# Last attention stage with two convolutions first, FFN transposes on two PSUM banks, shorter softmax bookkeeping

## The chip, the cores and the metric

The kernel runs on one core of a Trainium2 chip. The metric is the device time of one execution in microseconds, 1619.86 us before the change (median of 3 runs). The engines are TensorE (PE, with weight loads shown as PEld), VectorE (DVE), ScalarE (ACT), GpSimd (POOL) and the sync engine (SP), which here issues every DMA.

## The reference, cut to what matters

```
x  = x + attn(cond(x, c))            # stage A: per-sample mixing, then a state-space block
x  = x + ffn(cond2(x, c))            # stage B, the part touched, with the end of stage A

attn:  proj = h @ in_proj.T;  xBC = silu(causal conv of 4 taps)
       y = scan over 32 positions + x * D          # 64 heads in 8 groups
       yn = y * rsqrt(mean over the group of y*y + eps) * norm_weight * silu(gate)
       out = yn @ out_proj.T
cond2: conv1d(x, weight, 9 taps, 4 groups of 8 channels) + c @ c_weight.T + bias
ffn:   dots = softmax(x @ centroids.T / 0.1)       # 64 clusters
       hits = dots > 0.01
       query_sel = any(hits, axis=1);  row_sel = any(hits, axis=0)[assignments]
       out = where(query_sel & row_sel, x @ weight.T + bias, 0)
```

## The kernel before, in words

The 2048 rows (64 samples of 32 channels, 512 wide) lie in SBUF as 16 tiles of 128 rows, `acc[:, T]`. Every float32 product of the large matmuls is taken as three products of a high and a low part (`oh`/`ol`, `yh`/`yl`, `xh`/`xl`, `wh`/`wl`): ACT copies the high part out, DVE or POOL subtracts to get the low one.

Stage A is a loop over 32 stages n (a weight group by a half of the positions). A stage projects ten times on PE, and in the stage after it the four tiles i of stage n are finished: `Y(n, i)` (L675, the decay-weighted products on PE), `y_dve` (L692 y, L700 y times gate, on DVE), `y_high` (L719, ACT), `y_low` (L735, POOL), `y_square` (L711, ACT), `y_sum` (L726 and L730, POOL), `S` (L743, PE), `rstd` (L751 DVE, L756 POOL), `O(n, i)` (L775, twelve matmuls on PE, needs `yh` and `yl` of the tile) and `add_out` (L788, DVE). `A_dve` (L645) and `M_dve` (L655) on DVE make `dtx` and `Mb`, which `Y` reads. Stage 31 has no stage after it. `last_products` does this work, mixed with the start of stage B.

Stage B runs over the 16 tiles T. The updated rows are stored to HBM (`x2s`, L961) and loaded back shifted (`load_G`, L976, four DMAs of about 260 KB a tile); `conv2(T)` (L1058) and `conv2_last_tap` (L1066) are the convolution, always two tiles together; `x3_act` (L1076, ACT) adds the bias; `turn(T)` (L1085) transposes the tile in four pieces into PSUM bank `PT`; `x3_split` (L1094 ACT, L1096 DVE) makes high and low parts; `ffn(T, c)` (L1121, twelve matmuls) multiplies, c=1 the right 224 columns with the 64 cluster columns, c=0 the left 288; `ffn_ops` on DVE and ACT does the softmax over the clusters (L1147 row maximum, L1149 scale, L1154 exp on ACT, L1135 `dense` that copies the product out with its bias, L1159 reciprocal, L1161 scaling, L1164 running maximum `pmx`, L1165 row maximum, L1167 row mask `qs`). Up to tile 9 both halves of a tile are multiplied in its turn; from tile `LATE` = 10 only c=1 is, and the c=0 halves follow when the cluster mask is known: `ffn(10, 0)`, a transpose of `pmx` (L1253), its maximum and threshold (L1255, L1257), and two one-hot matmuls that spread the mask over the columns (L1261, L1262). After those, DVE and POOL put the masked results into `acc` (L1278, L1286, L1289, L1297, L1299) and SP stores them (L1272).

Nothing is scheduled by a planner: each engine runs its instructions in the order in which the Python calls append them to its queue, and waits at the written `wait` lines for an event of another engine, or of itself. So the order of calls in `last_products` and `second` is the order on every engine at once. SP's queue before the conv loads of tiles 0, 2, 1, 3 holds nothing of this place: `load_G(1)` and `load_G(3)` wait for projection 8 of stage 31, and the loads of tiles 4 and 5 for the convolutions of tiles 0 and 1, whose buffers they overwrite.

The names of PSUM banks: `PT` = 6 and `PG` = 3; `PG` holds the scan's small products and the sums of `S` until `rstd` has read them.

Of the kernel before, what the change touches and what calls it, by code (L numbers as in the profile page):

```python
# [10 lines left out]
AX = mybir.AxisListType  # L11

NT = 16
# [43 lines left out]
def adaln_attn_ffn_kernel(nc, x, emb, gin, b2, wbank, biask, w_in, w_dt, w_out, prm, cst, cw4, ctxw,  # L57
                          w_ffn, b_ffn, asg, x2s, out):
    ctx = ExitStack()
    with ctx:  # L60
# [58 lines left out]
        pmx = gmt[:, 2, :]  # L119
# [957 lines left out]

        def turn(T):
            pe.wait("x3", T)
            if T >= 1:  # L1080
                pe.wait("x3l", T - 1)
            else:
                pe.wait("dtx", (end_n, 3))
            for k in range(4):
                fn = lambda e, k=k: e.transpose(PS[:, PT, 128 * k:128 * k + 128], xs[:, T % 2, 128 * k:128 * k + 128], ident)  # L1085
                pe.op(fn, "xt", T) if k == 3 else pe.op(fn)

        def x3_split(T):
            act.wait("xt", T)
            if T >= LATE:  # L1090
                act.wait("O", (end_n, 3))
            elif T >= 3:
                act.wait("ff", (T - 3, 0))
            act.op(lambda e: e.copy(x3_slot(True, T), PS[:, PT, :]), "x3h", T)  # L1094
            dve.wait("x3h", T)
            dve.op(lambda e: e.tensor_tensor(x3_slot(False, T), PS[:, PT, :], f(x3_slot(True, T)), ALU.subtract), "x3l", T)  # L1096

        FB = ((SEG[0], PP[2]), PY)

# [37 lines left out]
        def ffn_ops(T):  # L1137
            r = T % 2
            banks = FB[r]
            lgt = PS[:, banks[1], 224:288]  # L1140
            nm, sx, rc = s4[:, 2 + r:3 + r], s4[:, 4 + r:5 + r], s4[:, 6 + r:7 + r]
            d = spots[T]
            dve.wait("ff", (T, 1))
            if T >= 1:
                dve.wait("fn", T - 1)
                dve.wait("q", T - 1)
            dve.op(lambda e: e.tensor_reduce(s4[:, 0:1], lgt, AX.X, ALU.max), "fm", T)  # L1147
            dve.wait("fm", T)
            dve.op(lambda e: e.tensor_scalar(nm, s4[:, 0:1], -10.0, None, ALU.mult), "fn", T)  # L1149
            act.wait("fn", T)  # L1150
            if T >= 2:
                act.wait("pm", T - 2)
                act.wait("qm", T - 2)
            act.op(lambda e: e.activation(ex[:, r, :], lgt, ACT.Exp, bias=nm, scale=10.0, accum_out=sx), "se", T)  # L1154
            dve.wait("ld_bf", 0)
            if T < LATE:
                dense(T, 0)
            dense(T, 1)
            dve.op(lambda e: e.reciprocal(rc, sx), "frc", T)  # L1159
            dve.wait("frc", T)  # L1160
            dve.op(lambda e: e.tensor_scalar(ex[:, r, :], ex[:, r, :], rc, None, ALU.mult), "pp", T)  # L1161
            dve.wait("pp", T)
            dve.wait("pm", T - 1)
            dve.op(lambda e: e.tensor_tensor(pmx, pmx, ex[:, r, :], ALU.max), "pm", T)  # L1164
            dve.op(lambda e: e.tensor_reduce(s4[:, 1:2], ex[:, r, :], AX.X, ALU.max), "qm", T)  # L1165
            dve.wait("qm", T)
            dve.op(lambda e: e.tensor_scalar(qs[:, T:T + 1], s4[:, 1:2], 0.01, None, ALU.is_gt), "q", T)  # L1167
            dve.wait("q", T)
            if T >= LATE:
                return  # L1170
            if T < APART:
                dve.op(lambda e: e.tensor_scalar(d, d, qs[:, T:T + 1], None, ALU.mult), "res", T)
                return
            dve.op(lambda e: e.scalar_tensor_tensor(out=d, in0=d, scalar=qs[:, T:T + 1], in1=acc[:, T, 4:516],
                                                    op0=ALU.mult, op1=ALU.add), "res", T)
# [23 lines left out]
        def last_products():  # L1199
            n = end_n  # L1200
            conv2(0)
            y_dve(n, 0)
            y_high(n, 0)
            y_low(n, 0)
            y_square(n, 0)
            y_sum(n, 0)
            A_dve(n, 2)
            A_dve(n, 3)
            M_dve(n, 2)
            M_dve(n, 3)  # L1210
            for i in (1, 2, 3):
                y_dve(n, i)
                y_square(n, i)
                y_sum(n, i)
                y_high(n, i)
                y_low(n, i)
            weights2(0)
            weights2(1)
            O(n, 0)
            Y(n, 2)  # L1220
            Y(n, 3)
            O(n, 1)
            S(n, (0, 1))
            conv2(1)
            conv2_last_tap(0)
            x3_act(0)
            load_G(4)
            load_G(5)
            O(n, 2)
            turn(0)  # L1230
            O(n, 3)
            S(n, (2, 3))
            x3_split(0)
            weights2(2)
            weights2(3)
            x3_act(1)
            for tiles in sums(n):
                rstd(n, tiles)
                for i in tiles:
                    add_out(n, i)  # L1240

        for n in range(NS):
            stage(n)
# [13 lines left out]
        dve.op(lambda e: e.tensor_scalar(csel, bc(sm[:, 40:41], 64, 128), 0.01, None, ALU.is_gt), "cs", 1)  # L1257
        pe.wait("cs", 1)
        pe.wait("oh1", 0)
        pe.wait("var", (end_n, 3))  # L1260
        pe.op(lambda e: e.matmul(PS[:, PG, :], csel, ohf, start=True, stop=True), "rsel", 0)  # L1261
        pe.op(lambda e: e.matmul(PS[:, PT, :], csel, ohf, start=True, stop=True), "rsel2", 0)  # L1262
        for T in range(LATE + 1, NT):
# [138 lines left out]
```

How the kernel before makes its waits and increments, by code:

```python
    def emit(self, eng, sems):  # L43
        seen = {}
        for it in self.items:
            if it[0] == "wait":
                v = self.book[it[1]][it[2]]
                if seen.get(it[1], 0) < v:
                    eng.wait_ge(sems[it[1]], v)
                    seen[it[1]] = v
            else:
                ins = it[1](eng)
                if it[2] is not None:
                    ins.then_inc(sems[it[2]], it[3])
```

## Time and profile before

| | us |
|---|---|
| median of 3 runs (1619.21 to 1621.07) | 1619.86 |
| the profiled execution, its own time | 1624.18 |
| its span, first to last instruction | 1622.4 |
| PE busy in the span | 1594.5 |
| stage 31's leftover work and first convolutions | about 1494 to 1521 |
| FFN turns | about 1521 to 1602 |
| mask, masked sums and stores | about 1602 to 1622 |

The span and the device time are of one profiled execution; the runs that the change is measured against have a median 4.3 us shorter than that execution. PE is busy for nearly all of the span, so a change shows where PE stands idle, and in the last 20 us, where PE is no longer the last to finish.

### The profile page before, as it was taken

The numbers are of one execution on the slowest core, as the hardware profiler recorded it, in microseconds if no ns is written. First come the engines' busy times: TensorE is split into PE (matmuls) and PEld (weight loads), VectorE is DVE, ScalarE is ACT, GpSimd is POOL, SyncE is SP. The second block draws the span as 40 slices with busy tenths as digits, with TensorE's granted clock in tenths as the row PEclk, the third lists the DMA queues.
The fourth block names the chain that finished last, engine by engine and source line by source line (L and its number), as shares of the span: only waits on it lengthen the run. The fifth ranks groups of instructions, "written<-read, shape, count | busy, mean of one in ns | idle before, by whom it ended". The sixth has DMA issues, their size and how long they took to land. (4 is left out here: it accounts for less than half of the span.)

```text
span 1622.4 us, 32566 instructions
## 1 busy us (share of the span) xinstructions
PE 1594.5 (98%) x13001; PEld 1279.6 (79%) x13001; DVE 1055.4 (65%) x1741; ACT 846.1 (52%) x1372; POOL 774.1 (48%) x731
## 2 busy tenths in 40 slices
PE   9999999999999999999999999999999999999997
PEld 6778888888888888877787888888888888887665
DVE  4877666665656666676786656565666666565456
ACT  3654556555555555555455655555454655554321
POOL 3564545546363644544345554636464554543203
PEclk9999999999999999999999999999999999999999
DMA  5110201111111102011012111111010201115782
GB/s 184 59 53 21 59 21 58 35 53 40 40 53 34 49 15 63 27 53 40 30 43 73 53 40 46 47 34 60 33 40 21 65 27 53 41 36 116 190 187 105
DMA packets 50294, 93.19 MB, mean 57 GB/s; under 512 B 5664, under 2 KB 6304, under 8 KB 50144
## 3 DMA queue, kind: packets, MB, share of 16 engines
q1 hardware_dynamic: 50144, 91.11, 19.5%
q8 instruction: 104, 1.70, 0.4%
q14 instruction: 46, 0.38, 0.1%
HBM read 82.64 MB, written 8.45 MB: 56 GB/s over the span
## 5 line engine op out<-in xcount | busy, mean ns | idle before, releaser
L487 PE MATMUL PS<-xh,wh 128*128 128x512 f32 x1280 | 519.6, 406 | 0.0
L487 PE MATMUL PS<-xh,wl 128*128 128x512 f32 x1280 | 499.8, 390 | 0.0
L487 PE MATMUL PS<-xl,wh 128*128 128x512 f32 x1280 | 499.8, 390 | 0.0
L522 DVE SCALAR_TENSOR_TENSOR cb<-PS,P,cb 128x496 f32<-128x496 f32 (+2 forms) x576 | 412.5, 716 | 132.4 <-ACT cb L508 118.8
L184 POOL TENSOR_TENSOR wl<-rw,wh 128x512 fp32r<-128x512 f32 x160 | 212.2, 1331 | 191.6 <-ACT wh L179 191.6
L726 POOL TENSOR_TENSOR ysum<-yq 128x256 f32<-128x256 f32 x128 | 109.5, 856 | 362.3 <-ACT yq L711 362.2
L487 PEld LDWEIGHTS PS<-xh,wl 128*128 128x128 f32 x1280 | 240.3, 188 | 52.9
L487 PEld LDWEIGHTS PS<-xh,wh 128*128 128x128 f32 x1280 | 240.6, 188 | 50.7 <-ACT wh L179 0.5
L487 PEld LDWEIGHTS PS<-xl,wh 128*128 128x128 f32 x1280 | 241.1, 188 | 44.4
L508 ACT ACTIVATE cb<-PS,P 128x512 f32<-128x512 f32 x192 | 148.4, 773 | 204.9 <-PE PS L487 204.9
L775 PE MATMUL PS<-oh,yh 128*128 128x512 f32 x512 | 200.1, 391 | 3.2 <-POOL yl L735 3.2
L655 DVE TENSOR_TENSOR big<-Lt,gmt 128x512 f32<-128x512 f32 x128 | 102.6, 843 | 153.3 <-ACT Lt L588 153.3
L775 PE MATMUL PS<-oh,yl 128*128 128x512 f32 x512 | 199.2, 389 | 0.0
L775 PE MATMUL PS<-ol,yh 128*128 128x512 f32 x512 | 199.2, 389 | 0.0
L711 ACT ACTIVATE yq<-y 128x512 f32<-128x512 f32 x128 | 81.0, 633 | 207.5 <-DVE y L692 201.2
L512 ACT ACTIVATE big<-PS 128x512 f32<-128x512 f32 x128 | 76.2, 595 | 147.9 <-PE PS L487 147.5
L542 ACT ACTIVATE big<-cb 128x512 f32<-128x512 f32 x192 | 119.6, 623 | 62.7 <-DVE cb L522 62.5
L788 DVE SCALAR_TENSOR_TENSOR acc<-PS,rs,acc 128x512 f32<-128x512 f32 x128 | 93.1, 749 | 84.0 <-issue 45.9
L756 POOL TENSOR_TENSOR rs<-vr,mh 128x1 f32<-128x1 f32 (+1 forms) x95 | 56.9, 599 | 168.6 <-DVE vr L751 168.5
L645 DVE TENSOR_TENSOR dtx<-PS,dtt 128x512 f32<-128x512 f32 x128 | 82.1, 682 | 59.9 <-PE PS L612 59.7
L775 PEld LDWEIGHTS PS<-oh,yh 128*128 128x128 f32 x512 | 96.1, 188 | 24.7 <-issue 5.1
L775 PEld LDWEIGHTS PS<-oh,yl 128*128 128x128 f32 x512 | 96.1, 188 | 20.0
(201 smaller groups left out, 2184.1 us busy)
## 6 DMA issues: line engine op xcount, KB each, us to landing
rw<-in_w_in SPq DMA_DIRECT2D x160, 256.0 KB, 2.7
ro<-in_w_out SPq DMA_DIRECT2D x64, 256.0 KB, 2.8
x2s<-acc SPq DMA_DIRECT2D x16, 260.0 KB, 5.3
out_x<-acc SPq DMA_DIRECT2D x16, 256.0 KB, 2.4
acc<-in_x SPq DMA_DIRECT2D x3, 1024.0 KB, 9.9
wh<-x2s SPq DMA_DIRECT2D x8, 260.0 KB, 3.4
wl<-x2s SPq DMA_DIRECT2D x8, 260.0 KB, 6.4
wh<-x2s SPq DMA_DIRECT2D x8, 259.5 KB, 4.2
```

Source lines behind the costliest of these rows:

```text
L184: pool.op(lambda e: e.tensor_tensor(wl[:, m, :], rw[:, q % RW, :], f(wh[:, m, :]), ALU.subtract), "w_lo", (u, m))
L487: fn = lambda e, k=k, w=w, v=v, i=i: e.matmul(PS[:, bank, :], w[:, m, 128 * k:128 * k + 128], v[:, k, a:a + 512], start=(i == 0), stop=(i ...
L508: act.op(lambda e: e.activation(cb[:, z % 2, :], PS[:, bank, :], ACT.Identity, bias=P[:, P_CB + c:P_CB + c + 1], scale=P[:, P_CW + 4 * c + ...
L512: act.op(lambda e: e.activation(gate[:, m - 6, :], PS[:, bank, :], ACT.Silu), "ev", (n, m))
L522: dve.op(lambda e, d=d, w=w: e.scalar_tensor_tensor(out=cv[:, :, d:32], in0=pv[:, :, 0:32 - d], scalar=w, in1=cv[:, :, d:32], op0=ALU.mult ...
L542: act.op(lambda e: e.activation(dst, cb[:, z % 2, :], ACT.Silu), "silu", (n, m))
L645: dve.op(lambda e: e.tensor_tensor(dtx[:, r, :].rearrange("p (j v c) -> p j v c", j=4, v=2), PS[:, b0:b0 + 2, 256 * r:256 * r + 256].rearr ...
L655: dve.op(lambda e: e.tensor_tensor(Mb[:, r], bc(Lt[:, 256 * i:256 * i + 256].rearrange("p (h o t) -> p h o t", h=8, o=1), 128, 8, 2, 32), ...
L711: act.op(lambda e: e.activation(yq[:, :], y[:, r, :], ACT.Square), "yq", (n, i))
L726: pool.op(lambda e: e.tensor_tensor(ysum[:, :], yq[:, 0:256], yq[:, 256:512], ALU.add), "ys1", (n, i))
L775: fn = lambda e, j=j, v=v, w=w, q=q: e.matmul(PS[:, O_bank(n, i), :], v[:, r, 128 * j:128 * j + 128], w[:, j, :], start=(q == 0), stop=(q ...
L788: dve.op(lambda e: e.scalar_tensor_tensor(out=acc[:, T, 4:516], in0=PS[:, O_bank(n, i), :], scalar=rs[:, i:i + 1], in1=acc[:, T, 4:516], o ...
```

## The change

`last_products` is rewritten: both first convolutions and their last tap come ahead of the first `O`, the elementwise work is done in pairs of tiles (0, 1) and (2, 3), the first transposes come before `O` of tile 2, and the splits of the FFN weights come after the second tile's output. `turn` writes to `PT` and `PG` in turn, and so waits for the split of the tile two before and not one before. In `ffn_ops` the scaling by the reciprocal and the running maximum are one instruction; the row mask is taken from the reciprocal itself (the largest exponential of a row is 1, so the largest softmax value is the reciprocal); and for the last tile `dense(15, 1)` is issued after the running maximum.

```
--- before.py
+++ after.py
@@ -1077,12 +1077,12 @@
 
         def turn(T):
             pe.wait("x3", T)
-            if T >= 1:
-                pe.wait("x3l", T - 1)
+            if T >= 2:
+                pe.wait("x3l", T - 2)
             else:
-                pe.wait("dtx", (end_n, 3))
+                pe.wait(*(("dtx", (end_n, 3)), ("var", (end_n, 3)))[T])
             for k in range(4):
-                fn = lambda e, k=k: e.transpose(PS[:, PT, 128 * k:128 * k + 128], xs[:, T % 2, 128 * k:128 * k + 128], ident)
+                fn = lambda e, k=k: e.transpose(PS[:, (PT, PG)[T % 2], 128 * k:128 * k + 128], xs[:, T % 2, 128 * k:128 * k + 128], ident)
                 pe.op(fn, "xt", T) if k == 3 else pe.op(fn)
 
         def x3_split(T):
@@ -1091,9 +1091,9 @@
                 act.wait("O", (end_n, 3))
             elif T >= 3:
                 act.wait("ff", (T - 3, 0))
-            act.op(lambda e: e.copy(x3_slot(True, T), PS[:, PT, :]), "x3h", T)
+            act.op(lambda e: e.copy(x3_slot(True, T), PS[:, (PT, PG)[T % 2], :]), "x3h", T)
             dve.wait("x3h", T)
-            dve.op(lambda e: e.tensor_tensor(x3_slot(False, T), PS[:, PT, :], f(x3_slot(True, T)), ALU.subtract), "x3l", T)
+            dve.op(lambda e: e.tensor_tensor(x3_slot(False, T), PS[:, (PT, PG)[T % 2], :], f(x3_slot(True, T)), ALU.subtract), "x3l", T)
 
         FB = ((SEG[0], PP[2]), PY)
 
@@ -1143,28 +1143,26 @@
             dve.wait("ff", (T, 1))
             if T >= 1:
                 dve.wait("fn", T - 1)
-                dve.wait("q", T - 1)
             dve.op(lambda e: e.tensor_reduce(s4[:, 0:1], lgt, AX.X, ALU.max), "fm", T)
             dve.wait("fm", T)
             dve.op(lambda e: e.tensor_scalar(nm, s4[:, 0:1], -10.0, None, ALU.mult), "fn", T)
             act.wait("fn", T)
             if T >= 2:
                 act.wait("pm", T - 2)
-                act.wait("qm", T - 2)
             act.op(lambda e: e.activation(ex[:, r, :], lgt, ACT.Exp, bias=nm, scale=10.0, accum_out=sx), "se", T)
             dve.wait("ld_bf", 0)
             if T < LATE:
                 dense(T, 0)
-            dense(T, 1)
+            if T < NT - 1:
+                dense(T, 1)
+            dve.wait("se", T)
             dve.op(lambda e: e.reciprocal(rc, sx), "frc", T)
             dve.wait("frc", T)
-            dve.op(lambda e: e.tensor_scalar(ex[:, r, :], ex[:, r, :], rc, None, ALU.mult), "pp", T)
-            dve.wait("pp", T)
             dve.wait("pm", T - 1)
-            dve.op(lambda e: e.tensor_tensor(pmx, pmx, ex[:, r, :], ALU.max), "pm", T)
-            dve.op(lambda e: e.tensor_reduce(s4[:, 1:2], ex[:, r, :], AX.X, ALU.max), "qm", T)
-            dve.wait("qm", T)
-            dve.op(lambda e: e.tensor_scalar(qs[:, T:T + 1], s4[:, 1:2], 0.01, None, ALU.is_gt), "q", T)
+            dve.op(lambda e: e.scalar_tensor_tensor(out=pmx, in0=ex[:, r, :], scalar=rc, in1=pmx, op0=ALU.mult, op1=ALU.max), "pm", T)
+            dve.op(lambda e: e.tensor_scalar(qs[:, T:T + 1], rc, 0.01, None, ALU.is_gt), "q", T)
+            if T == NT - 1:
+                dense(T, 1)
             dve.wait("q", T)
             if T >= LATE:
                 return
@@ -1199,45 +1197,48 @@
         def last_products():
             n = end_n
             conv2(0)
-            y_dve(n, 0)
-            y_high(n, 0)
-            y_low(n, 0)
-            y_square(n, 0)
+            conv2(1)
+            conv2_last_tap(0)
+            for i in (0, 1):
+                y_dve(n, i)
+                y_high(n, i)
+                y_low(n, i)
+                y_square(n, i)
             y_sum(n, 0)
+            y_sum(n, 1)
             A_dve(n, 2)
             A_dve(n, 3)
             M_dve(n, 2)
             M_dve(n, 3)
-            for i in (1, 2, 3):
-                y_dve(n, i)
-                y_square(n, i)
-                y_sum(n, i)
-                y_high(n, i)
-                y_low(n, i)
-            weights2(0)
-            weights2(1)
+            x3_act(0)
+            x3_act(1)
+            load_G(4)
+            load_G(5)
             O(n, 0)
             Y(n, 2)
             Y(n, 3)
             O(n, 1)
             S(n, (0, 1))
-            conv2(1)
-            conv2_last_tap(0)
-            x3_act(0)
-            load_G(4)
-            load_G(5)
+            turn(0)
             O(n, 2)
-            turn(0)
             O(n, 3)
             S(n, (2, 3))
+            for i in (2, 3):
+                y_dve(n, i)
+                y_high(n, i)
+                y_low(n, i)
+                y_square(n, i)
+            y_sum(n, 2)
+            y_sum(n, 3)
             x3_split(0)
-            weights2(2)
-            weights2(3)
-            x3_act(1)
-            for tiles in sums(n):
-                rstd(n, tiles)
-                for i in tiles:
-                    add_out(n, i)
+            rstd(n, (0, 1))
+            add_out(n, 0)
+            add_out(n, 1)
+            for k in range(4):
+                weights2(k)
+            rstd(n, (2, 3))
+            add_out(n, 2)
+            add_out(n, 3)
 
         for n in range(NS):
             stage(n)
@@ -1257,7 +1258,6 @@
         dve.op(lambda e: e.tensor_scalar(csel, bc(sm[:, 40:41], 64, 128), 0.01, None, ALU.is_gt), "cs", 1)
         pe.wait("cs", 1)
         pe.wait("oh1", 0)
-        pe.wait("var", (end_n, 3))
         pe.op(lambda e: e.matmul(PS[:, PG, :], csel, ohf, start=True, stop=True), "rsel", 0)
         pe.op(lambda e: e.matmul(PS[:, PT, :], csel, ohf, start=True, stop=True), "rsel2", 0)
         for T in range(LATE + 1, NT):
```

PE in the last stage, as a difference (L675 is `Y` of tiles 0 and 1, L1058 the convolution, L1066 its last tap, L775 the first `O`; `w` is `w4`; a row with x8 is eight matmuls):

```order
 L675 MATMUL PS<-big,dtx 64x64 x32
-L1058 MATMUL PS<-wh,w 32x512 x8
+L1058 MATMUL PS<-wh,w 32x512 x16
+L1066 MATMUL PS<-wh,w 32x512 x8
 L775 MATMUL PS<-oh,yh 128x512
 L775 MATMUL PS<-ol,yh 128x512
```

The convolution of tile 1 and the last taps of both tiles now stand ahead of `O` of tile 0; before, they stood behind `O` of tile 1.

DVE in the same place (`big` in L692 is `xsd`, in L700 `gate`, in L655 the tile `Mb`; `yg` and `big` in L700 are the two buffers of `ygb`):

```order
 L692 TENSOR_TENSOR y<-PS,big 128x512
 L700 TENSOR_TENSOR yg<-y,big 128x512
-L645 TENSOR_TENSOR dtx<-PS,dtt 128x512 x2
-L655 TENSOR_TENSOR big<-Lt,gmt 128x512 x2
-L692 TENSOR_TENSOR y<-PS,big 128x512
-L700 TENSOR_TENSOR big<-y,big 128x512
+L692 TENSOR_TENSOR y<-PS,big 128x512
+L700 TENSOR_TENSOR big<-y,big 128x512
+L645 TENSOR_TENSOR dtx<-PS,dtt 128x512 x2
+L655 TENSOR_TENSOR big<-Lt,gmt 128x512 x2
 L692 TENSOR_TENSOR y<-PS,big 128x512
```

The y and gate products of tile 1 now come ahead of the two `A_dve` and two `M_dve`, four instructions earlier.

POOL in the same place, before:

```order
L735 TENSOR_TENSOR yl<-yg,yh 128x512
L726 TENSOR_TENSOR ysum<-yq 128x256
L730 TENSOR_TENSOR big<-ysum 128x128
L726 TENSOR_TENSOR ysum<-yq 128x256
L730 TENSOR_TENSOR big<-ysum 128x128
L735 TENSOR_TENSOR yl<-big,yh 128x512
```

and now:

```order
L735 TENSOR_TENSOR yl<-yg,yh 128x512
L735 TENSOR_TENSOR yl<-big,yh 128x512
L726 TENSOR_TENSOR ysum<-yq 128x256
L730 TENSOR_TENSOR big<-ysum 128x128
L726 TENSOR_TENSOR ysum<-yq 128x256
L730 TENSOR_TENSOR big<-ysum 128x128
```

The low part of tile 1 now stands ahead of both sums of squares.

DVE in a late FFN turn (`gmt` is `ex` or `pmx`, `s` one column of `s4`):

```order
 L1135 TENSOR_TENSOR big<-PS,pb 128x224
 L1159 RECIPROCAL s<-s 128x1
-L1161 TENSOR_SCALAR gmt<-gmt,s 128x64
-L1164 TENSOR_TENSOR gmt<-gmt 128x64
-L1165 TENSOR_REDUCE s<-gmt 128x1
-L1167 TENSOR_SCALAR qs<-s 128x1
+L1162 SCALAR_TENSOR_TENSOR gmt<-gmt,s 128x64
+L1163 TENSOR_SCALAR qs<-s 128x1
 L1096 TENSOR_TENSOR ol<-PS,oh 128x512
```

Four instructions between the reciprocal and the next tile's low part became two.

## Rows read from the trace of the kernel before

**Rows 1.** The page, part 1: busy time by engine.

```profile
PE 1594.5 (98%) x13001; PEld 1279.6 (79%) x13001; DVE 1055.4 (65%) x1741; ACT 846.1 (52%) x1372; POOL 774.1 (48%) x731
```

**Rows 2.** Windows: stretch, length, busy by engine, then clock, DMA share, GB/s.

```profile
1540.00:1560.00 20.00, 20.00 (x179) 12.71 (x179) 9.92 (x34) 5.57 (x15) 0.00 (x0) 1.00 0.97 215
```

**Rows 3.** Timeline of PE, last stage: start, duration, line, idle before in brackets.

```profile
1493.95 1.93 PE L1058 MATMUL PS<-wh,w 128*32 128x512 f32 x16
1497.60 0.47 PE L775 MATMUL PS<-oh,yh 128*128 128x512 f32 x1 [1.72 <-POOL yl L735]
...
1500.51 1.16 PE L675 MATMUL PS<-big,dtx 64*64 64x64 f32 x64
1503.18 0.47 PE L775 MATMUL PS<-oh,yh 128*128 128x512 f32 x1 [1.51 <-POOL yl L735]
...
1508.30 1.09 PE L1066 MATMUL PS<-wh,w 32*32 32x512 f32 x16
```

**Rows 4.** Timeline of DVE, last stage, and all of L700 (ns min/median/max).

```profile
1494.09 0.69 DVE L692 TENSOR_TENSOR y<-PS,big 128x512 f32<-128x512 f32 x1 [0.94 <-PE PS L675]
...
1495.42 1.28 DVE L645 TENSOR_TENSOR dtx<-PS,dtt 128x512 f32<-128x512 f32 x2
1496.62 2.58 DVE L655 TENSOR_TENSOR big<-Lt,gmt 128x512 f32<-128x512 f32 x2
...
L700 DVE TENSOR_TENSOR yg<-y,big x64: 691/692/1648, 77.7 to 1502.5; 128x512 f32<-128x512 f32 x64
```

**Rows 5.** Timeline of POOL, last stage.

```profile
1496.23 1.26 POOL L735 TENSOR_TENSOR yl<-yg,yh 128x512 fp32r<-128x512 f32 x1 [12.05 <-ACT yh L719]
```

**Rows 6.** SP issues of load_G(1), time to landing (window 1489.9:1490.4), all of `x2s`.

```profile
1488.69 1.73 SPq L976 DMA_DIRECT2D wh<-x2s  x4
...
wh<-x2s SPq DMA_DIRECT2D x1, 258.5 KB, 5.6
...
DMA to landing us min/median/max: 3.1/5.9/10.9
```

**Rows 7.** Timeline of PE, late FFN turns.

```profile
1583.52 0.63 PE L1085 MATMUL PS<-C,big 128*128 128x128 f32 x4 [0.53 <-DVE ol L1096]
1583.91 0.38 PE L1121 MATMUL PS<-xh,oh 128*128 128x288 f32 x1
...
1595.97 0.63 PE L1085 MATMUL PS<-C,big 128*128 128x128 f32 x4 [0.62 <-DVE yl L1096]
...
1598.73 0.40 PE L1121 MATMUL PS<-xh,yh 128*128 128x288 f32 x1 [0.53 <-DVE yl L1096]
...
1602.78 0.30 PE L1253 MATMUL PS<-C,gmt 128*64 128x128 f32 x1 [0.60 <-DVE gmt L1164]
```

**Rows 8.** Timeline of DVE, turns 12, 13 and 15.

```profile
1592.90 0.21 DVE L1147 TENSOR_REDUCE s<-PS 128x1 f32<-128x64 f32 x1
...
1594.27 0.26 DVE L1161 TENSOR_SCALAR gmt<-gmt,s 128x64 f32<-128x64 f32 x1
...
1595.14 0.69 DVE L1096 TENSOR_TENSOR yl<-PS,yh 128x512 fp32r<-128x512 f32 x1
...
1600.83 0.23 DVE L1147 TENSOR_REDUCE s<-PS 128x1 f32<-128x64 f32 x1
...
1601.71 0.39 DVE L1135 TENSOR_TENSOR dtx<-PS,pb 128x224 f32<-128x224 f32 x1 [0.47 <-ACT gmt L1154]
...
1602.50 0.23 DVE L1164 TENSOR_TENSOR gmt<-gmt 128x64 f32<-128x64 f32 x1
```

**Rows 9.** The chain that ended last, its end: start, us, what.

```profile
1605.80 0.60 ACT y L1305
...
1611.68 6.25 POOL acc L1289 x5
1617.93 1.22 POOLq L60
```

**Rows 10.** Window of three us, PE only: busy, clock, DMA share, GB/s.

```profile
1606.00:1609.00 3.00, 3.00 (x14) 0.50 0.45 175
```

## Prediction

> **What bounds the kernel now.** I read the page's first part, then the windows, then PE's timeline where the windows show it idle, then DVE, POOL and SP at those places, and last the chain that ended last. PE is busy for 98% of the span [rows 1], so only time in which PE stands idle, or in which something else is last, can be won. The middle of stage B has no such time: 20.00 of 20 us busy [rows 2]. The transposes of tiles 2 to 11 wait for nothing there, and the shorter DVE work of these turns is worth nothing. Two places are left.
>
> First, stage 31's leftover: PE idles 1.72 us before `O` of tile 0 and 1.51 us before `O` of tile 1, both times for the low part `yl` made on POOL [rows 3]. That is 3.23 us, and behind it PE runs without a gap to the late turns.
>
> Second, the late turns with only half a product: 0.53 us before the transpose of tile 12, 0.62 before that of tile 15, 0.53 before `ffn(15, 1)`, 0.60 before the transpose of `pmx` [rows 7]; the transpose of tile 14 has a gap like these. Each is a wait for the newest low part or for the running maximum, which DVE makes. After the mask PE is busy only because late products are left over: the chain ends in ACT's copy of the mask, POOL's sums to 1617.93 and a last 1.22 us of waiting for the store [rows 9]. That tail has unchanged operations and starts from the mask, so whatever brings the mask earlier brings the end earlier by as much.
>
> **Last stage.** PE executes the same matmuls; the second convolution (1.93 us, less 0.07 of overlap, from the first one's row) and the last taps (1.09 less 0.07) go into the first gap [rows 3]: 2.9 us of work in place of 1.72 of idling. The step needs four things.
>
> *The data of tile 1.* Its loads are issued from 1488.69 on, four within 1.73 us; the last, issued at about 1490.0, takes 5.6 us to land [rows 6], so 1495.6. The first convolution leaves PE at 1495.8. The cost is 0; the other end is a landing that is late by the semaphore's way and the other loads behind it, for which I take 0.3. What is queued behind this wait on PE is all of `O`, `Y` 2 and 3, and through them every engine.
>
> *`dtx` of tiles 2 and 3, which `O` of tile 0 waits for.* DVE's y (0.69) and gate product (0.69) of tile 1 now stand ahead of it. From 1495.42 [rows 4]: y to 1496.1, gate product to 1496.8, `dtx` twice (1.28) to 1498.1, `Mb` twice at the slow 2.58 to 1500.7. PE comes to `O` at 1495.8 + 1.86 + 1.02 = 1498.7, and to `Y` of tile 2 at 1501.6. Nothing is late. The bound is a gate product at its slowest, 1.65 us [rows 4]: 0.96 later, which makes `O` wait 0.5.
>
> *The low part of tile 1.* Its `yh` follows the gate product (1496.8) by the ACT copy, about 0.7, and `yl` takes 1.26 [rows 5], so 1498.8; `O` of tile 1 comes at 1502.7. The second gap of 1.51 goes entirely.
>
> *The low part of tile 2, next in turn to be late.* `Y` 2 and 3 end at about 1502.8, DVE starts y right behind. From y of tile 0 (1494.09 [rows 4]) to the first `O` (1497.60 [rows 3]) took 3.51 us: 1502.95 + 3.51 = 1506.46. PE, after `O` of tile 1 and the sums (3.26, from 1503.18 to the convolution 1.86 ahead of the taps at 1508.30 [rows 3]) and the transposes of tile 0 (0.39 [rows 7]), comes at 1506.45. So 0 again, with no slack; if POOL is held up, up to 0.6 is lost. The later steps (`yl` of tile 3, the split of tile 0, the rsqrt, the splits of the FFN weights, the sum of `rstd` that frees bank PG for the transpose of tile 1) come out 0.6 us or more ahead of PE by the same adding up, and their slack covers ACT's later `x3_split`.
>
> SP gains an earlier place for the loads of tiles 4 and 5 (behind the taps, 1498.7, not 1509.4). They queue behind loads and stores that are already issued, and are needed 20 us later. Nobody waits.
>
> Sum of this place: -3.23, plus 0.3 that I put in for the three slacks of a few tenths: -2.9. Bounds -3.5 (small spaces around the gaps that the modelled ends of matmuls hide) and -1.8 (0.3, 0.5 and 0.6 all paid).
>
> **Late turns.** With two banks the transposes of tiles 12 and 14 no longer wait for the low part of the tile before. They are done (0.39 from transpose to product [rows 7]) while that low part is made. That is worth 0.39 once: with tile 12, ahead of two convolutions on PE. For tile 14 the same happens, but the low part of tile 14 is held by DVE's own queue. There the step is 1592.90 to 1595.14 and again to the next [rows 8], 2.84 a turn (2.24, and 0.60 for the low part), against 2.1 for PE's transposes (0.39) and product (about 1.7, half of the 3.45 below). Of the four operations from the scaling at 1594.27 to the low part at 1595.14, 0.87 us, two remain, with one wait in place of three; I take 0.42, as half of it. The fused operation has no row: with the two remaining at a fifth of the time, 0.7 would be saved; with the fused one as dear as the two it replaces, 0.2; with all as dear as the four, nothing. Two turns (low parts of tiles 14 and 15) give 2 x 0.45 = 0.90. Then `ffn(15, 1)` starts at 1598.73 - 0.39 - 0.90 = 1597.44. Behind it stand its own product and `ffn(10, 0)`, to 1602.18 before, 3.45 us in all [rows 7], so 1600.89. The running maximum of tile 15: the maximum starts about 2.0 after the product's start (the product must be done), then before it took 1.90 (1600.83 to 1602.73 [rows 8]); less `dense` (0.39) and one of the two operations (0.27), 1.24. That is 3.24, under 3.45: PE is last, and the gap of 0.60 goes. `dense(15, 1)` falls into the 0.4 us of the transpose of `pmx`.
>
> Sum of this place: -0.39 - 0.90 - 0.60 = -1.89. Bounds: -1.0 (the two operations as long as the four) and -2.4 (0.7 twice).
>
> **Sum.** -2.9 - 1.9 = -4.8 us. From the profiled execution's 1624.18 that is 1619.4; from the median of the runs, 1619.86, which the next measurement stands against, 1615.1. This measurement can tell 0.2%, 3.2 us, from no change.
>
> **The clock.** PE's granted clock is 0.50, so 1.2 of 2.4 GHz, in 1606 to 1609 [rows 10], after PE had idled for the mask. DVE and POOL set the end there, so I put neither gain nor loss on it.
>
> **The lock.** DVE's two `Mb` products took 2.58 us beside POOL's `yl`, [rows 4, 5], against a gate product's usual 0.69 for the same size. The longest gate product, 1.65, would fit it too. As a mechanism of this kernel: of a DVE product with both inputs in SBUF and a POOL subtraction, the later waits out the earlier. Now the gate product of tile 1 (1496.1) meets `yl` of tile 0 (1496.2), and that of tile 3 (1505.0) meets `yl` of tile 2 (1505.1). If POOL wins the first, `dtx` is 0.96 late and `O` waits 0.5 to 0.8; if DVE wins the second, `yl` of tile 2 is 0.6 late and PE waits 0.5. Together the change would give 1.3 less: 1616.4. The Trainium skill, SBUF — State Buffer, "Who interferes with whom", states this rule: the port pair that VectorE and GpSimd share is an exclusive lock, and a VectorE instruction with two SBUF inputs contends with a GpSimd one that reads SBUF. By that rule the trace agrees in kind (2.58 for two); which instruction comes first is open.
>
> **The rivals.**
> - *The lock costs* at both places: 1616.4. For it the 2.58 us; against it that both meetings are within 0.1 us and may fall the good way. 14%.
> - *Another wait takes the place of the stall in the last stage*: the pairs make ACT square tile 1 only after POOL's first sum, and put tile 3's work and the split of tile 0 behind it. If the chain gate product, `yl`, sums, split, `rstd` runs 3 us late, only the late turns gain: 1618.0. Against it are slacks of 0.6 us and more. 7%.
> - *The late turns don't shorten*, because ACT's exponentials and copies are as long as DVE's row: only the first place, 1617.0. Against it, DVE waits 0.47 for ACT in a turn [rows 8] and is busy for the rest. 7%.
> - *Slower: the data of tile 1 come late.* PE now stands at the loads with everything behind it. At the longest landing of any transfer of `x2s` in the trace, 10.9 us [rows 6], they would be there at 1500.9, 5.1 after PE. A gap so long could halve the clock as it does at the end, where it is 0.50 for 3 us [rows 10] and so gives away half of that, 1.5 us. -4.8 + 5.1 + 1.5 = +1.8: 1621.7. It is slower from a landing 4.8 us late, or 3.3 with the clock. Against it stand the 5.6 us read for this very load, whose place in SP's queue is unchanged. 4%.
> - *The change doesn't do what it says*: the orders of PE, DVE and POOL do change as shown; that the time doesn't, 2%.
>
> **How the numbers follow.** The forecast holds 66%, with its own range 1614.0 to 1617.1, both places at their bounds; 3 of these 66 lie above 1616.6. Faster by over 0.2% is below 1616.6: 0.63 of the forecast and 0.09 of the lock case, 0.72. Same: the rest of both, either place lost, half of the late data, and no effect, 0.26. Slower: the other half of the late data, 0.02. The range for 8 in 10 is 1613.8, just under the forecast's own, to 1618.0, where the last stage gives nothing.
>
> **What would show it.** PE's timeline: the tap of tiles 0 and 1 ends near 1498.8 and `O` follows at once; a first gap at 1495.8 shows late data, one at 1498.8 shows `dtx`, one at 1506.5 the low part of tile 2. The first `ffn` starts near 1518.3, not 1521.2. In the late turns the low parts of DVE are 2.4 apart, not 2.84, and the transpose of `pmx` has no gap before it. A PE gap in 1520 to 1580, or POOL idle between its sums after 1606, would show me wrong.

## The result, and the profile after

The changed kernel takes 1613.53 us (median of 6 runs, 1612.93 to 1615.37), the kernel before 1619.13 in the same rounds: the ratio is 0.9965, 95% interval 0.9954 to 0.9976, so 3.9 to 7.4 us less. Timed again later it was 0.9956 (0.9943 to 0.9968). I had said 1615.1, range 1613.8 to 1618.0. The direction and both places were right. The time lies 0.27 us under the range: the change is -5.6, not -4.8, and the kernel before came out at 1619.13, the median of the three runs that I started from and three more, 0.73 below the 1619.86 that I set the change against.

The two profiled executions differ by 11.0 us of span, more than the change is worth. So I compare stretches of the program, not times from the span's start. The first convolution of the last stage starts at 1493.95 before [rows 3] and here at 1488.74, with the same code ahead of it; those 5.2 us are the start of the program, told at the end.

PE's timeline in the last stage of the changed kernel (start, duration, line, idle before in brackets), answering to [rows 3]:

```profile
1488.74 1.93 PE L1058 MATMUL PS<-wh,w 128*32 128x512 f32 x16
1491.10 1.93 PE L1058 MATMUL PS<-wh,w 128*32 128x512 f32 x16 [0.43 <-DMA wh<-x2s]
1492.96 1.09 PE L1066 MATMUL PS<-wh,w 32*32 32x512 f32 x16
1493.98 0.50 PE L775 MATMUL PS<-oh,yh 128*128 128x512 f32 x1
...
1497.99 0.50 PE L775 MATMUL PS<-oh,yh 128*128 128x512 f32 x1
...
1501.21 0.64 PE L1085 MATMUL PS<-C,big 128*128 128x128 f32 x4
1502.11 0.47 PE L775 MATMUL PS<-oh,yh 128*128 128x512 f32 x1 [0.27 <-issue]
...
1513.09 0.38 PE L1121 MATMUL PS<-xh 128*128 128x288 f32 x1
```

Both gaps of 1.72 and 1.51 are gone: the first `O` follows the taps at once, and the second follows `Y` at once. New are 0.43 of waiting for the data of tile 1 and 0.27 ahead of `O` of tile 2. From the first convolution to the first FFN product it is 24.35 us; before it was 27.25.

DVE and POOL in the same place, answering to [rows 4, 5]:

```profile
1490.93 0.69 DVE L700 TENSOR_TENSOR big<-y,big 128x512 f32<-128x512 f32 x1
...
1492.74 2.37 DVE L655 TENSOR_TENSOR big<-Lt,gmt 128x512 f32<-128x512 f32 x2
...
1500.18 0.69 DVE L700 TENSOR_TENSOR big<-y,big 128x512 f32<-128x512 f32 x1
```

```profile
1491.03 1.75 POOL L735 TENSOR_TENSOR yl<-yg,yh 128x512 fp32r<-128x512 f32 x1 [12.05 <-ACT yh L719]
1492.75 1.81 POOL L735 TENSOR_TENSOR yl<-big,yh 128x512 fp32r<-128x512 f32 x1
...
1500.28 1.73 POOL L735 TENSOR_TENSOR yl<-yg,yh 128x512 fp32r<-128x512 f32 x1 [2.49 <-ACT yh L719]
```

Twice a gate product starts 0.10 us ahead of a low part, keeps its 0.69, and the low part takes 1.75 and 1.73 in place of 1.26. The low part of tile 1 starts with the two `Mb` products, and both are long: 1.81, and 2.37 for the two.

The late turns, PE and then DVE, answering to [rows 7, 8]:

```profile
1574.66 0.60 PE L1085 MATMUL PS<-C,big 128*128 128x128 f32 x4
1575.26 0.40 PE L1121 MATMUL PS<-xh,oh 128*128 128x288 f32 x1
...
1589.15 0.40 PE L1121 MATMUL PS<-xh,yh 128*128 128x288 f32 x1 [0.51 <-DVE yl L1096]
...
1592.54 0.30 PE L1254 MATMUL PS<-C,gmt 128*64 128x128 f32 x1
```

```profile
1585.66 0.28 DVE L1162 SCALAR_TENSOR_TENSOR gmt<-gmt,s 128x64 f32<-128x64 f32 x1
1585.86 0.15 DVE L1163 TENSOR_SCALAR qs<-s 128x1 f32<-128x1 f32 x1
1586.04 0.69 DVE L1096 TENSOR_TENSOR yl<-PS,yh 128x512 fp32r<-128x512 f32 x1
...
1588.40 0.69 DVE L1096 TENSOR_TENSOR yl<-PS,yh 128x512 fp32r<-128x512 f32 x1
```

The transposes no longer wait; low parts are 2.36 apart, before 2.84; the transpose of `pmx` has no gap. From the transpose of tile 11 to that of `pmx` it is 19.98 us, before 22.05. From there to the end of POOL nothing changed. But the last wait of SP, for the last store, did. SP's waits in the last 30 us, before and after:

```profile
SPq L60 <- DMA out_x<-acc: 2.5, 1, 2.5
```

```profile
SPq L60 <- DMA out_x<-acc: 1.7, 1, 1.7
```

From POOL's end to the span's it is 3.25 us before and 2.50 after. That was in no term of my sum. The four stretches give -2.90, -0.06, -2.07 and -0.75, together -5.8.

The same stretches in every profiled execution, each worked out from that kernel's timeline. They repeat to 0.1 us where the whole time does not, but for the first, which moves with the data of tile 1. The stretch after POOL is good to 0.05, and in `e_tail`, where POOL has one sum less, it is no measure of the end:

| kernel | ratio to before, interval | first conv. to first FFN | to transpose 11 | to `pmx` | POOL's end to the end | loads on q14 |
|---|---|---|---|---|---|---|
| before | | 27.25 | 59.53 | 22.05 | 3.25 | 46 |
| before_again | | 27.25 | 59.50 | 22.06 | 3.21 | 46 |
| changed | 0.9965 (0.9954 to 0.9976) | 24.35 | 59.47 | 19.98 | 2.50 | 45 |
| after_again | 0.9956 (0.9943 to 0.9968) | 23.73 | 59.50 | 19.97 | 2.52 | 45 |
| e_stage | 0.9981 (0.9972 to 0.9990) | 24.05 | 59.47 | 22.04 | 3.25 | 46 |
| e_banks | 0.9996 (0.9987 to 1.0005) | 27.26 | 59.53 | 21.59 | 3.24 | 46 |
| e_softmax | 0.9986 (0.9977 to 0.9994) | 27.27 | 59.47 | 20.85 | 2.47 | 45 |
| e_dense | 0.9999 (0.9990 to 1.0008) | 27.29 | 59.51 | 21.74 | 3.24 | 46 |
| e_conv | 0.9992 (0.9983 to 1.0001) | 25.35 | 59.52 | 22.06 | 3.31 | 46 |
| e_pad_dve | 0.9967 (0.9954 to 0.9979) | 23.95 | 59.53 | 19.95 | 3.23 | 46 |
| e_pad_act | 0.9957 (0.9943 to 0.9971) | 23.71 | 59.47 | 19.95 | 2.46 | 45 |
| e_lock | 0.9954 (0.9940 to 0.9967) | 23.52 | 59.53 | 19.99 | 2.53 | 45 |
| e_tail | 0.9959 (0.9947 to 0.9972) | 23.72 | 59.48 | 19.95 | 3.67 | 45 |
| e_lateload | 1.0000 (0.9989 to 1.0010) | 30.20 | 59.47 | 19.95 | 2.54 | 45 |

### The profile page after: what moved, and what is told of

Read it like the earlier page. It is cut to its first block, busy times and chain, and to the rows that moved or that the text cites. A ratio compares the mean times of both kernels' runs of the same rounds, so it can differ in the third digit from the quotient of the medians.

```text
span 1611.4 us, 32541 instructions
## 1 busy us (share of the span) xinstructions
PE 1586.3 (98%) x13001; PEld 1273.4 (79%) x13001; DVE 1049.9 (65%) x1709; ACT 846.0 (53%) x1372; POOL 775.1 (48%) x731
## 4 chain that ended last, share of the span: by engine, by line
PE 84%; ACT 6%; DVE 4%; issue 3%; POOL 2%; DMA 0%; POOLq 0%; SPq 0%; DVEq 0%; ACTq 0%
PE PS L487 48%; PE PS L775 20%; PE PS L675 4%; PE PS L612 3%; PE PS L1121 2%; ACT L588 2%; PE PS L1058 2%; DVE cb L522 1%; ACT big L549 1%; PE PS L743 1%; ACT Lt L588 1%; PE PS L359 1%; PE PS L624 1%; PE PS L208 1%; ACT oh L191 1%
## 5 line engine op out<-in xcount | busy, mean ns | idle before, releaser
L655 DVE TENSOR_TENSOR big<-Lt,gmt 128x512 f32<-128x512 f32 x128 | 102.3, 841 | 153.4 <-ACT Lt L588 153.4
L775 PE MATMUL PS<-oh,yh 128*128 128x512 f32 x512 | 200.0, 391 | 0.3 <-issue 0.3
L775 PE MATMUL PS<-ol,yh 128*128 128x512 f32 x512 | 199.2, 389 | 0.0
L775 PE MATMUL PS<-oh,yl 128*128 128x512 f32 x512 | 199.2, 389 | 0.0
L775 PEld LDWEIGHTS PS<-oh,yh 128*128 128x128 f32 x512 | 96.1, 188 | 21.0 <-issue 0.8
L775 PEld LDWEIGHTS PS<-oh,yl 128*128 128x128 f32 x512 | 96.1, 188 | 19.9
```

What stands on the lines that cost most here:

```text
L655: dve.op(lambda e: e.tensor_tensor(Mb[:, r], bc(Lt[:, 256 * i:256 * i + 256].rearrange("p (h o t) -> p h o t", h=8, o=1), 128, 8, 2, 32), ...
L775: fn = lambda e, j=j, v=v, w=w, q=q: e.matmul(PS[:, O_bank(n, i), :], v[:, r, 128 * j:128 * j + 128], w[:, j, :], start=(q == 0), stop=(q ...
```

## The experiments: the parts one by one

**The last stage alone.** Kernel before with the new `last_products`.

> Kernel before with the new last_products alone (transposes on one bank, FFN turns as before). Theory, each place gives what its own PE gaps held: the stretch from the first convolution to the first FFN product is 24.35 us, 2.9 shorter than before's 27.25, and the late turns stay at 22.05, so -2.9 in all. Rival, the stretch is shorter only together with the two banks: 25 us or more. Rival, the end after the mask shortens for any change (0.76 us in the changed kernel's profile): -3.6.

24.05 and 22.04: the place gives 3.2 us by itself and the late turns nothing. In this execution both convolutions take 3.96 together, where they take 3.64 in `after_again`: the missing 0.3 of the 3.5 found there is again waiting for data. The end stays at 3.25, so it doesn't shorten for any change.

**Two banks alone.** Kernel before with

```
-            if T >= 1:  pe.wait("x3l", T - 1)
+            if T >= 2:  pe.wait("x3l", T - 2)
...
-   ... PS[:, PT, ...]
+   ... PS[:, (PT, PG)[T % 2], ...]
```

> Kernel before with the transposes on two banks alone. Theory: the last stage as before (27.2 us, or up to 0.3 more, since the transpose of tile 1 now waits for the sum that frees bank PG); the late turns 0.39 shorter, 21.66 from the transpose of tile 11 to that of pmx, because DVE's queue holds all the later low parts. Rival, the late turns hang on the transposes: four times 0.39, 20.5.

21.59: 0.46 less, near the 0.39. PE's waits in its late turns (waiter, waited for, total, times, longest) show where the rest of the waiting went:

```profile
PE PS L1121 <- DVE yl L1096: 1.5, 2, 1.0
PE PS L1261 <- DVE csel L1257: 0.7, 1, 0.7
PE PS L1253 <- DVE gmt L1164: 0.6, 1, 0.6
```

The transposes (L1085) are off the list, and two products (L1121) wait in their place, 1.5 together and 1.0 at most. The rival is out.

**The shorter softmax alone.** Kernel before with the fused running maximum and the mask from the reciprocal:

```
-  tensor_scalar(ex, ex, rc, MULT); wait; tensor_tensor(pmx, pmx, ex, MAX)
-  tensor_reduce(s4, ex, MAX); wait; tensor_scalar(qs, s4, 0.01, IS_GT)
+  scalar_tensor_tensor(pmx, in0=ex, scalar=rc, in1=pmx, MULT, MAX)
+  tensor_scalar(qs, rc, 0.01, IS_GT)
```

> Kernel before with the fused running maximum and the row mask from the reciprocal alone, dense of tile 15 at its old place. Theory: low parts 2.36 to 2.42 apart in place of 2.84. With one bank, PE's transpose waits for the low part and its product for nothing: turns of tiles 14 and 15 save 0.45 each, the one before the two last convolutions 0, and the running maximum of tile 15 about 0.27: late turns 22.05 - 1.17 = 20.9. Rival, the fused operation is as dear as the two: 21.5 or more.

20.85, as the theory had it; its own timeline has the fused operation at 0.28, and the low parts of tiles 13 and 14 2.36 apart. And the end is 2.47 here: the short end comes with this part.

**The last `dense` alone.** `dense(15, 1)` behind the running maximum, else as before.

> Kernel before with dense of tile 15 behind the running maximum, alone. Theory: it takes 0.39 off the chain that ends in the transpose of pmx, whose gap of 0.60 has room for it: late turns 21.66. Rival, the waits around it cost as much: 22.05.

21.74, so 0.31 less, but 0.19 comes back: `csel` is later, since `dense` now stands ahead of it on DVE. In the changed kernel it does not come back (1.96 from the `pmx` transpose to the second mask product, L1262, as before; 2.15 here). The parts give -0.46, -1.20 and -0.31, together -1.97, against -2.07 to -2.10 for all.

**PE's move without the pairs.** Kernel before with `conv2(1)` and `conv2_last_tap(0)` called right behind `conv2(0)`.

> Kernel before with the second convolution and the last taps of tiles 0 and 1 moved ahead of the first O, and nothing else: the elementwise work stays in its old order. Theory, the move of PE's work is nearly the whole gain of the last stage: the first gap goes, and the second shrinks from 1.51 to about 0.4, since O of tile 0 comes 1.1 later while yl of tile 1 comes when it did: stretch from first convolution to first FFN product 24.1 to 24.4, against 23.7 with the full reordering where the data are in time, 27.25 before. Rival, the pairs are what removes the second gap: 25.2 or more.

25.35: neither. The move of the convolution gives 1.90 of the 3.5. My theory had one gap left, and there are three, 1.64 in all; from PE's timeline:

```profile
1499.00 0.47 PE L775 MATMUL PS<-oh,yh 128*128 128x512 f32 x1 [0.54 <-POOL yl L735]
...
1502.93 0.47 PE L775 MATMUL PS<-oh,yh 128*128 128x512 f32 x1 [0.62 <-ACT yh L719]
...
1509.58 0.58 PE L743 MATMUL PS<-C,big 128*128 128x1 f32 x4 [0.48 <-DVE vr L751]
```

The second row names ACT's copy, but the copy for tile 2 had been done since 1500.59. What ends at 1502.82, 0.11 ahead of this `O`, is POOL's low part of tile 2, which the old order starts only behind POOL's two sums for the same tile (1499.96 and 1500.79). The third is a sum matmul that waits for bank PG, which the old order frees late. So the rest of the reordering is worth 1.6 on top, which I had put at 0.4 to 0.7. What of it is due to the pairs and what to the earlier `rstd`, the transposes and the weight splits no run separates.

## The experiments: what the sum had missed

**The end.** The page of before counts 46 instruction loads on q14, the page of the changed kernel 45. One of the 46 lies in the last 6 us. The DMA view of before in 1616.4 to 1619.4, packets and share by queue, and the stores issued there with their time to landing:

```profile
q1 hardware_dynamic: 625, 1.13, 99.7%
q14 instruction: 1, 0.01, 0.6%
...
out_x<-acc SPq DMA_DIRECT2D x4, 256.0 KB, 3.0
```

The same stretch before the end of the changed kernel (1605.4 to 1608.4) has no such load:

```profile
q1 hardware_dynamic: 624, 1.15, 100.4%
...
out_x<-acc SPq DMA_DIRECT2D x5, 256.0 KB, 2.6
```

If the 32 instructions that DVE lost are the reason, 32 harmless ones must bring it back:

```
+            if T < LATE:
+                for _ in range(4 if T < 2 else 3):
+                    c = P_CW + next(spare)
+                    dve.op(lambda e, c=c: e.memset(P[:, c:c + 1], 0.0))
```

> The changed kernel with 32 one-column fills added on DVE, three or four in each of the turns 0 to 9, where PE never waits for DVE. In the changed kernel one instruction load on queue q14 fewer is seen than before (45, not 46), and it is the one that lay in the last 6 us; from the end of POOL to the end of the span it takes 2.50 us, before 3.25. Theory, the shorter list of DVE moved that load out of the last stores: with as many instructions as before it comes back (46) and the end is 3.25 again; all else equal, so 0.75 us over the changed kernel. Rival, the shorter end is the luck of the profiled executions or another effect of the softmax code: 2.50 stays.

And the control, the same on ACT:

> Control: the changed kernel with 32 one-column copies added on ACT in the same turns. Theory, the load in the last 6 us is DVE's: the end stays 2.50, unless ACT's own loads are shifted into it. Rival, any 32 instructions bring it back: 3.25.

With 32 fills on DVE the end is 3.23 and there are 46 loads, one of them again in the same stretch (1607.8 to 1610.8 of that execution):

```profile
q1 hardware_dynamic: 622, 1.13, 100.2%
q14 instruction: 1, 0.01, 0.6%
...
out_x<-acc SPq DMA_DIRECT2D x4, 256.0 KB, 3.0
```

With 32 copies on ACT the end is 2.46, with 45. All thirteen executions with POOL's own order of sums fall into one of the two groups: 46 and 3.2 to 3.3, or 45 and 2.5. The 0.75 us are shown to hang on the length of DVE's instruction list. Where they are lost, the landings of the last stores in the traces say. In the changed kernel the last eight land 0.62 to 0.72 apart. Before, the load starts 3.42 us before the end, takes 0.31, and the store that lands next comes 1.12 behind the one before it; the last one comes 0.95 behind, the others 0.67 to 0.72. So about 0.4 goes at the load and 0.25 at the last store, and `before_again` and the run with the fills show both again (1.11 and 0.93, 1.10 and 0.97). The load meets a saturated queue (about 100% of the engines' time). Why 0.31 us of one load costs more than itself, and why the last store pays too, no run shows.

**The data of tile 1.** Loads of tile 3 issued first:

```
-        load_G(1)
         load_G(3)
+        load_G(1)
```

> The changed kernel with the loads of tile 3 issued ahead of those of tile 1. Theory, the second convolution stands at its data with no slack (0.43 us of waiting in the changed kernel): 1 MB at about 220 GB/s and 1.9 us of issuing bring the data 4 to 5 us later, and all of it is lost on PE: first convolution to first FFN product 28.5 to 29.5 us in place of 24.35. Rival, the work behind has slack against DVE and POOL and gives part of it back: 27 or less. Should the gap halve PE's clock, 1.5 more.

30.20, 6.5 more than where the data are in time: the 28.5 to 29.5 that I expected, with most of the 1.5 for the clock on top. PE's timeline and two windows (us, PE busy, clock, DMA share, GB/s):

```profile
1488.38 1.93 PE L1058 MATMUL PS<-wh,w 128*32 128x512 f32 x16
1495.23 3.26 PE L1058 MATMUL PS<-wh,w 128*32 128x512 f32 x16 [4.92 <-DMA wh<-x2s]
```

```profile
1493.00:1495.00 2.00, 0.00 (x0) 0.89 1.06 236
1495.00:1496.00 1.00, 0.77 (x4) 0.50 1.01 373
```

The wait is 4.92, and the convolution behind it runs at the granted clock of 0.50, 1.2 GHz, for 3.26 instead of 1.93: the slower rival of my prediction, with its clock term (1.3 for my 1.5), in its own experiment. The ratio is 1.000: the whole gain is gone. Nothing behind gave any of it back.

**The lock.** Gate product of tile 3 held until the low part of tile 2 is done: `if z == 4 * NS - 1: dve.wait("yl", (n, 2))`.

> The changed kernel with DVE's gate product of tile 3 held until POOL's low part of tile 2 is done. In the changed kernel the gate product (1500.18, 0.69 us) meets that low part (1500.28), which takes 1.73 in place of 1.26, and PE then idles 0.27 ahead of O of tile 2. Theory, the earlier of the two holds up the other: the low part takes 1.26 to 1.30 again, the 0.27 goes, and the gate product's delay falls into slack: stretch 23.45. Rival, the low part is long for another reason (ACT's copy, the transposes): 1.73 and 23.7 stay; or the delayed tile 3 is late for its O: over 23.7.

POOL's timeline:

```profile
1501.96 1.29 POOL L737 TENSOR_TENSOR yl<-yg,yh 128x512 fp32r<-128x512 f32 x1 [1.92 <-ACT yh L721]
1504.80 1.29 POOL L737 TENSOR_TENSOR yl<-big,yh 128x512 fp32r<-128x512 f32 x1 [1.56 <-ACT yh L721]
```

1.29 again, no gap ahead of `O` of tile 2, stretch 23.52, against 23.71 to 23.73 in three executions of the other order. The mechanism holds; the 0.2 us can't be told in the whole time (0.9954 beside 0.9956). By its profile alone it is the best version here. Since 0.26 or 0.27 is waited at this `O` in every other execution of the new order, the last stage without any wait is worth 3.7.

**The tail.** The last tile's sum on DVE:

```
-            pool.op(... tensor_tensor(acc, acc, d, ALU.add), "add", T)
+            eng, kind = (dve, "fin") if T == NT - 1 else (pool, "add")
+            eng.op(... tensor_tensor(acc, acc, d, ALU.add), kind, T)
```

> The changed kernel with the last tile's sum on DVE, not on POOL. In the changed kernel POOL works without a pause from 1596.22 to 1608.9 in ten operations of 1.27 us, DVE ends at 1606.66. Theory, POOL's own row of sums sets the end: POOL ends 1.25 earlier (1607.7) and DVE's last sum ends at 1607.4; end 1.2 us earlier. Rival, the stores of the last four tiles are the bound: nothing, or under 0.4.

POOL ends 1.20 earlier, and the end of the span comes 0.04 earlier: the rival. Two rows say why, the last of DVE's timeline and the DMA queue in the last 6 us:

```profile
1605.92 1.56 DVE L1290 TENSOR_TENSOR acc<-acc,dtx 128x512 f32<-128x512 f32 x1
```

```profile
GB/s 382 355 383 382 410 369 383 355 423 355 396 369 396 355 410 369 383 382 396 382 369 355 396 382 396 328 423 410 396 342 382 396 396 355 82 0 0 0 0 0
```

DVE's sum meets POOL's and takes 1.56, not the 0.75 that I had counted on. But the last store is still issued 0.6 us earlier than in the changed kernel, counted back from the end, and it lands 0.67 behind the one before it, the spacing of the last stores in the changed kernel too (0.62 to 0.72). The stores fill the queue at about 380 GB/s for the last 5 us. So the queue holds the end, and neither POOL's row nor DVE's late sum does.

**Both kernels once more.** Is 24.35 the changed kernel's own number, and do the other three repeat?

> The changed kernel once more. Theory, the stretches from the first convolution on repeat within 0.1 (late turns 19.95, end after POOL 2.5, 45 instruction loads on q14); the stretch of the last stage is 23.7, or more by what the data of tile 1 are late in that execution (24.35 at a wait of 0.43). The time of the first 30 us differs from execution to execution. Rival, 24.35 is this kernel's own: it comes back.

> The kernel before once more. Theory, the first convolution of the last stage starts near 1488.5 or 1490.8, not at 1493.95: the profiled execution of before had a start of the program that was 5.2 us slower than that of the changed kernel, where the code is the same; 27.25, 59.5, 22.05 and 3.25 repeat. Rival, the unchanged part is slower in the kernel before: 1493.95 comes back.

The changed kernel gives 23.73, 59.50, 19.97 and 2.52, so 24.35 was not its own number. The 0.62 between them is the data wait, which comes and goes; the profile shows 0.43 of it as a gap, and the rest is hidden in the space around it. The kernel before gives 27.25, 59.50, 22.06 and 3.21, with 46 loads, and its first convolution at 1488.88. The changed kernel against the one before by stretches is then -3.52, 0.00, -2.09 and -0.69, together -6.3, with the data in time.

## Why the prediction was right or wrong, point by point

- *What bounds.* Right as to the two places on PE. The end moved besides (see the tail below). The middle is 59.5 us in every kernel, so the shorter DVE work is worth nothing there.
- *Last stage, -2.9.* The mechanism was right, the size too small: where the data come in time it is -3.5 (23.73 for 27.25), the bound that I gave and set down as "small spaces around the gaps". Without the 0.26 that is still waited at `O` of tile 2 it is -3.7 (`e_lock`). The gaps were put at 3.23. The distance of starts [rows 3] minus the work gives 1.79 and 1.58 for the gaps that the profile calls 1.72 and 1.51, and there was a third gap: "behind it PE runs without a gap to the late turns" isn't so. Before the sums of tiles 2 and 3 (1515.68) PE waits 0.13 by the profile and 0.28 by the starts, and in the changed kernel it doesn't. The three make 3.65, and where the last 0.1 lies I don't know. That the profiled execution gives exactly -2.90 is luck: in it the larger gaps are paid back by 0.62 for data and 0.27 at `O`, against the 0.3 that I put in for waits.
- *The data of tile 1, cost 0 to 0.3.* Too narrow: 0 in most executions, 0.2 to 0.3 in two, 0.62 in the profiled one. That nothing is in reserve there, `e_lateload` shows.
- *The low part of tile 2, next to be late.* It is the next to be late, by 0.27 where the sum had 0, and for the reason named in the lock: DVE wins both meetings. So of the rival in which the lock costs at both places the second half came true, at 0.27 and not 0.5, and the first didn't. By the Trainium skill, SBUF — State Buffer, "Who interferes with whom", the later one blocks until the first is done; here the gate product's 0.69 less its lead of 0.10 is 0.59, and the low part is 0.47 to 0.49 longer, so the trace agrees to about 0.1. `e_lock` agrees: apart from each other they take 0.69 and 1.29.
- *Late turns, -1.89.* -2.07 to -2.10. Two banks were taken at 0.39 and give 0.46, the chain's step at 2.39 and it is 2.36.
- *The tail.* This is the step that failed: "That tail has unchanged operations and starts from the mask, so whatever brings the mask earlier brings the end earlier by as much." Its operations are unchanged, but the last store lands 0.75 earlier, since one instruction load of DVE no longer lies among the stores. I put that at nothing, from a chain that ends in POOL's sums; what holds the end is the queue of the stores, which `e_tail` shows, and a load in that queue costs. No range of mine had a place for it. With it the stretches add up to -6.3, from 1619.86 to 1613.6, under the range; without it they give -5.6 and 1614.3, inside.
- *The clock.* I put neither gain nor loss on it, and that holds. Three us of PE behind the mask ran at 0.50 before (14 matmuls) [rows 10], and at 1.00 in the same place of the changed kernel (25):

```profile
1595.80:1598.80 3.00, 3.00 (x25) 1.00 0.45 175
```

  From the transpose of `pmx` to POOL's end it is 16.37 before and 16.36 after all the same.
- *From profile to median.* I set the change against 1619.86, the median of three. The same kernel has since had medians of 1619.13 to 1621.26. Most runs fall into two groups about 2 us apart, by what happens at the start of the program (last section), so three runs don't fix the base to better than a microsecond, more than the 0.27 by which the range missed. Taken group by group the change is 5.8 and 5.9 us in the first rounds and 6.7 and 6.9 in those of `after_again`, on either side of the 6.3 of the stretches. The -5.6 lies inside my bounds of the change itself (-5.9 to -2.8).

## What to carry to other kernels

Where one engine is busy 98% of the time, the worth of a reordering is the distance of starts minus the work between them, and independent work put in a gap pays only with the producers behind it reordered too: here 1.9 of 3.5 us came from the move and 1.6 from the rest of the reordering. Cut a chain's operations where that chain is last, and check the very end for what the instruction count does to it. When the profiled executions differ by more than the change, compare stretches between two landmarks of the same code.

## What the runs showed of the hardware

- Thirty-two short instructions fewer on DVE shift its instruction loads. One that fell among saturated stores cost 0.75 us at the end, and 32 dummy ones on DVE brought it back; 32 on ACT didn't.
- The start of the program differs between executions of the same kernel. In the profiled execution of before PE runs at half speed for the first 28.8 us. Four transposing products of the first tile (eight instructions) take 2.07 there and 1.16 in that of the changed kernel. PE's timeline, first of the execution of before, then of the changed kernel:

```profile
14.98 2.07 PE L359 MATMUL PS<-bd,acc 128*128 128x128 f32 x8
```

```profile
14.63 1.16 PE L359 MATMUL PS<-bd,acc 128*128 128x128 f32 x8
```

The granted clock reads 1.00 for this stretch in both, but the trace of before holds no clock record at all ahead of 28.80, and that of the changed kernel none ahead of 14.16, and just there the matmuls fall to half their time. A stretch without a record is printed as 1.00, so ahead of the first record the reading says nothing. `before_again`, with the code of before, has its first record at 9.80, 1.16 for the same products and its first convolution at 1488.88: the 5.2 us were this. What decides when PE comes to full speed no run shows.
- The two groups of runs go with something else, and there the clock does show it. In four of the 14 profiled executions (`e_stage`, `e_softmax`, `e_pad_dve`, `e_lock`) PE waits 3.1 to 3.4 us for an ACT operation at about 37 us, and the clock is at 0.50 for 6.8 us there; their first convolution comes near 1491, not at 1488 to 1490, and each of them took a time of the upper group. PE's timeline and one window, of `e_stage` and then of `before_again`:

```profile
37.95 0.66 PE L624 MATMUL PS<-big 128*32 128x32 f32 x32 [3.35 <-ACT big L542]
36.00:42.00 6.00, 4.05 (x40) 0.50 0.02 8
```

```profile
36.34 0.46 PE L624 MATMUL PS<-big 128*32 128x32 f32 x32 [1.69 <-ACT big L542]
36.00:42.00 6.00, 5.66 (x57) 1.00 0.32 110
```

- A gap of 4.9 us on PE was followed by a granted clock of 0.50 and a convolution of 3.26 us for 1.93. Gaps of 1.7 us in the last stage were followed by none. But the length of the gap alone doesn't tell: near the start one of 1.65 us in `after_again` was followed by 0.50 for 3.4 us, and the one of 1.69 us in `before_again` above wasn't.
